# First gate/up tile decoded in the prologue, and the second norm rebuilt on transposes in two pairs of banks

## What is computed

```python
x = _layernorm(x + attention(x, weight_qkv, weight_proj))          # the "batch" axis of x is its second one
x = _layernorm(x + selective_scan(ctx_1024, z=x, in_proj_w, conv_w, conv_b, x_proj_w,
                                  dt_proj_w, dt_proj_b, A_log, D))
x = _layernorm(x + down(silu(gate(x)) * up(x)))
```

## Time and profile before

| | |
|---|---|
| median of 3 runs | 992.76 us (992.56 to 994.16) |
| profiled execution | 990.59 us, span 988.8 us |
| mean granted TensorE clock | 0.906 of full speed |
| busy: PE, DVE, ACT, POOL | 88%, 77%, 68%, 49% |

### The profile page before, as it was taken

The page is one execution under the profiler, slowest core; times in us unless marked ns, Lnnn a source line. Parts: engine busy times, 40 slices in busy tenths (PEclk is TensorE's granted clock), DMA queues, the critical chain, the costliest instruction groups (busy, mean ns, idle before and its releaser), DMA issues.

```text
span 988.8 us, 11890 instructions
## 1 busy us (share of the span) xinstructions
PE 869.3 (88%) x3824; PEld 626.4 (63%) x3824; DVE 765.2 (77%) x1066; ACT 672.4 (68%) x994; POOL 481.3 (49%) x445
## 2 busy tenths in 40 slices
PE   6879888787878897787989879899999999899997
PEld 3547654465544674456545457787777778688885
DVE  3797899877998879986788666888888888355442
ACT  4698985789956899668696464777777776242321
POOL 0079867799767998669676631221112111001000
PEclk9789777999779797787979988999999999899998
DMA  8167979589996799967999222111111110223221
GB/s 259 39 168 177 209 161 229 117 221 245 210 224 122 204 241 210 224 125 202 208 289 277 83 96 86 46 61 42 42 42 44 62 42 22 75 86 107 86 64 53
DMA packets 49908, 135.99 MB, mean 138 GB/s; under 512 B 5364, under 2 KB 13684, under 8 KB 41156
## 3 DMA queue, kind: packets, MB, share of 16 engines
q0 software_dynamic: 8064, 58.72, 30.9%
q1 hardware_dynamic: 40432, 76.44, 23.1%
q10 hardware_dynamic: 1364, 0.25, 0.2%
HBM read 57.93 MB, written 78.51 MB: 138 GB/s over the span
## 4 chain that ended last, share of the span: by engine, by line
PE 26%; issue 23%; DVE 23%; ACT 19%; POOL 5%; DMA 4%; DVEq 1%; ACTq 0%; POOLq 0%; SPq 0%
DVE state L1191 6%; PE banks L606 5%; ACT decay L893 5%; PE banks L720 5%; ACT scaled L882 5%; PE banks L744 4%; DVE leaf L1219 3%; DVE w_gu L1219 3%; PE banks L644 3%; PE banks L548 3%; DVE conv_in L1094 3%; POOL state L1442 2%; ACT leaf L1001 2%; DMA hT<-y_scratch 2%; DMA y_scratch<-state 1%
## 5 line engine op out<-in xcount | busy, mean ns | idle before, releaser
L1442 POOL TENSOR_TENSOR state<-state,crep 128x512 f32<-128x512 f32 x243 | 334.8, 1603 | 85.9 <-DVE state L1191 79.7
L1191 DVE TENSOR_TENSOR_SCAN state<-decay,banks 128x512 f32<-128x512 f32 x243 | 280.7, 1202 | 54.2 <-PE banks L644 44.6
L720 PE MATMUL banks<-x2T,wgu 128*128 128x512 f32 x1056 | 246.3, 393 | 4.8 <-DVE hT L1270 4.1
L644 PE MATMUL banks<-ident,scaled 128*128 128x128 f32 x1024 | 175.9, 314 | 69.1 <-DVE state L1191 49.7
L720 PEld LDWEIGHTS banks<-x2T,wgu 128*128 128x128 f32 x1056 | 197.9, 189 | 52.1 <-DVE hT L1270 11.3
L644 PEld LDWEIGHTS banks<-ident,scaled 128*128 128x128 f32 x1024 | 136.2, 161 | 143.1 <-DVE state L1191 63.4
L893 ACT ACTIVATE decay<-delta,negA 128x512 f32<-128x512 f32 x256 | 169.9, 722 | 77.6 <-DVE state L1191 69.8
L882 ACT ACTIVATE scaled<-duT,BT 128x512 f32<-128x512 f32 x256 | 163.8, 720 | 0.0
L1001 ACT ACTIVATE leaf<-idx_sb,table,table_gap 128x1024 f32<-128x1024 uint8 (+1 forms) x132 | 129.4, 1022 | 6.8 <-DVE w_down L1219 3.2
L1219 DVE COPY_PREDICATED leaf<-idx_sb,leaf 128x1024 f32<-128x1024 uint8 (+1 forms) x88 | 94.1, 1069 | 7.1 <-issue 6.1
L1534 POOL TENSOR_TENSOR pool_wait_here<-minus_half 128x1 f32<-128x1 f32 x22 | 4.3, 193 | 180.6 <-DVE w_gu L1219 116.2
(11 more groups left out here) (140 smaller groups left out, 1155.6 us busy)
## 6 DMA issues: line engine op xcount, KB each, us to landing
y_scratch<-state POOLq DMA_DIRECT2D x52, 1024.0 KB, 8.5
crep<-c_scratch SPq DMA_DIRECT2D x64, 256.0 KB, 5.4
idx_sb<-in_idx SPq DMA_DIRECT2D x11, 512.0 KB, 3.5
xT_sb<-in_xT SPq DMA_DIRECT2D x16, 256.0 KB, 4.8
y_scratch<-u SPq DMA_DIRECT2D x4, 1024.0 KB, 6.1
y_scratch<-state SPq DMA_DIRECT2D x4, 1024.0 KB, 6.3
leaf<-x_scratch SPq DMA_DIRECT2D x16, 256.0 KB, 2.8
out<-leaf SPq DMA_DIRECT2D x16, 256.0 KB, 2.0
```

Source lines behind the costliest of these rows:

```text
L644: last = nc.tensor.transpose(banks[:, k % NB, lc * LQ:(lc + 1) * LQ], scaled[:, g % SR, lc, et * P:(et + 1) * P], ident[:])
L720: last = mm(banks[:, 2 * tb + w, :], wgu[par][:, w, ws, t * P:(t + 1) * P], x2T[:, tb, xs, t, :], start=t == 0 and n == 0, stop=t == HT - ...
L1191: V.tensor_tensor_scan(state[:, g % GR, et, :], decay[:, k % DR_RING, :], banks[:, k % NB, :], 0.0, ALU.mult, ALU.add).then_inc(scan_ready, 1)
L1442: G.tensor_tensor(state[:, g % GR, et, :], state[:, g % GR, et, :], crep[:, g % CR, :], ALU.mult)\
```

## The change

- *Prologue.* SP loads the table first and the first index tile (0.5 MB) after xT, ahead of `wqkv`. POOL computes the table's gaps and then all eight leaves of gate/up tile 0 into the still unused `state`; DVE does the two bit operations after the taps of et 0 and 1, six selects before `softplus` and the seventh after it. SP stores the tile in DRAM (`w0_scratch`) and loads it back into `w_gu` when the scan's buffers are free. Before the in-projections PE runs four matmuls on zeros (`WARM`).
- *End of the scan.* The last row of y gets a place of its own (`y_last`, in `leaf`) and is loaded at n = 11, behind a wait for `y_out` and ahead of the last `repeat_c`; both index tiles leave that place.
- *Second norm.* `y_over` only transposes y (8 per half) into one pair of banks, 0 and 1 for the first four halves, 4 and 5 for the last four; DVE adds x1 from SBUF and takes the statistics there. `x2_over` has the pair 2 and 3, then 6 and 7. All four row gatings are DVE's. ACT copies half k before it applies half k + 1. The decode of tile 1 moves to the end of the stage, the first block of the FFN's first tile is cut in halves of 12 matmuls between the halves of the norm, and the silu and product of its first two blocks move ahead of the next decode.

The core of the diff (declarations and renumbered semaphores left out):

```diff
+                sp.dma_start(first_table, lut.to_broadcast([P, 16])).then_inc(first_lut_in, 16)
                 sp.dma_start(ip[:], ipT.rearrange("(t p) n -> p t n", p=P)).then_inc(ip_in, 16)
                 load_ctx(0)
                 load_xT(0)
+                sp.dma_start(first_words, idx[0, :, 0:2 * H]).then_inc(first_idx_in, 16)
                 sp.dma_start(wqkv[:], wqkvT.rearrange("(t p) n -> p t n", p=P)).then_inc(wqkv_in, 16)
...
+                        if n == 0 and b == 0:
+                            sp.wait_ge(first_mux_ready, 7)
+                            sp.dma_start(w0_scratch, first_leaf(0)).then_inc(first_stored, 16)
...
                         if b == S - 1 and n == 11:
                             sp.dma_start(table[:], lut.to_broadcast([P, 16])).then_inc(lut_in, 16)
-                            load_idx(*FIRST)
-                            load_idx(*SECOND)
+                            sp.wait_ge(y_out, 16)
+                            sp.dma_start(y_last, y_scratch[b].rearrange("(p t) l -> p t l", p=P)).then_inc(y_in[b], 16)
...
-                load_row(S - 1)
+                sp.dma_start(x1b[S - 1][:, 0:3, :], x1_scratch[S - 1].rearrange("(t p) h -> p t h", p=P)[:, 0:3, :])\
+                    .then_inc(x1_in[S - 1], 16)
+                sp.wait_ge(first_stored, 16)
+                sp.dma_start(w_gu[:].rearrange("p w n -> p (w n)"), w0_scratch).then_inc(first_in, 16)
+                load_idx(*SECOND)
+                load_idx("down", 0)
                 store_x2(0)
                 store_x2(1)
-                chunk_done(*FIRST)
-                load_idx("down", 0)
...
+                pe.wait_ge(zeros_ready, 1)
+                for _ in range(WARM):
+                    mm(banks[:, 7, :], state[:, 0, 0, 0:P], state[:, 0, 0, :], start=True, stop=True)
                 pe.wait_ge(ip_in, 16)
...
-                        mm(banks[:, half_bank(k, i), :], ident[:], x1_tile(b, lt), start=True, stop=False)
-                        for et in range(4):
-                            last = mm(banks[:, half_bank(k, i), et * P:(et + 1) * P],
-                                      yb[b][:, et, lt * P:(lt + 1) * P], ident[:], start=False, stop=et == 3)
-                        last.then_inc(sum_out, 1)
+                        if k % S:
+                            pe.wait_ge(x1y_ready, 2 * k - 1 + i)
+                        for et in range(ET):
+                            last = nc.tensor.transpose(banks[:, y_bank(k, i), et * P:(et + 1) * P],
+                                                       yb[b][:, et, lt * P:(lt + 1) * P], ident[:])
+                        last.then_inc(yT_out, 1)
...
-                residual(0)
-                residual(1)
-                for k in range(6):
-                    residual(k + 2)
+                y_over(0)
+                rest_summed()
+                y_over(1)
+                for k in range(2 * S):
+                    if k + 2 < 2 * S:
+                        y_over(k + 2)
                     x2_over(k)
-                gate_up(0, 0, (0,), first=True)
-                x2_over(6)
-                gate_up(0, 0, (1,), first=True)
-                x2_over(7)
+                    if 3 <= k < 7:
+                        gate_up(0, 0, ((k - 3) // 2,), first=True, halves=((k - 3) % 2,))
                 gate_up(0, 0, (2, 3), first=True)
...
                     for i, lt in enumerate(lts):
-                        A(x1b[b][:, lt, :], banks[:, half_bank(k, i), :], ACT.Identity, bias=shift[:, lt:lt + 1],
+                        A(x1b[b][:, lt, :], x1b[b][:, lt, :], ACT.Identity, bias=shift[:, lt:lt + 1],
                           scale=rstd[:, lt:lt + 1]).then_inc(x2_ready, 1)
...
+                for k in range(2 * S):
+                    x2T_hi(k)
+                    if k == 2:
+                        act.wait_ge(gap_ready, 1)
+                        act.wait_ge(ysum_out, ET * (DS * S - G0) + ET)
+                    if k in WITH_HALF:
+                        leaves(*SECOND, WITH_HALF[k])
+                    if k + 1 < 2 * S:
+                        norm_apply(k + 1)
+                leaves(*SECOND, (4, 5, 6))
+                silus(0, 0)
+                silus(0, 1)
                 high_part(1, 1)
...
                     for i, lt in enumerate(lts):
-                        dve.wait_ge(sum_out, 2 * k + i + 1)
-                        V.bn_stats(stats[:, lt, :], banks[:, half_bank(k, i), :]).then_inc(stat2_ready, 1)
+                        dve.wait_ge(yT_out, 2 * k + i + 1)
+                        V.tensor_tensor(x1b[b][:, lt, :], banks[:, y_bank(k, i), :], x1_tile(b, lt), ALU.add)\
+                            .then_inc(x1y_ready, 1)
+                    for i, lt in enumerate(lts):
+                        dve.wait_ge(x1y_ready, 2 * k + i + 1)
+                        V.bn_stats(stats[:, lt, :], x1b[b][:, lt, :]).then_inc(stat2_ready, 1)
...
+                first_selects(range(6))
                 softplus(0, (0, 1))
                 softplus(0, (2, 3))
+                first_selects((6,))
                 head_products(0, 3)
...
+                for j in range(8):
+                    G.tensor_tensor(first_wait[:, 8 + j:9 + j], minus_half[:, 0:1], minus_half[:, 0:1], ALU.add)
+                    G.tensor_scalar(first_leaf(j), first_bit(0), first_gap[:, j:j + 1], first_table[:, 2 * j:2 * j + 1],
+                                    ALU.mult, ALU.add).then_inc(first_leaf_ready, 1)
```

More of the change, by code:

```diff
@@ L161, in layer @@
         OWN_FROM = 3
+        WARM = 4
         DOWN = (3, 2, 1)
@@ L329, in loads_of @@
             if kind == "gate_up":
[L330 to L331 removed]
+                return f
+            return f + 1
         def wide(kind):
@@ L708, in x2_over, with gate_up @@
                             last.then_inc(x2T_out, 1)
-                def gate_up(f, par, blocks=range(TB), first=False):
+                def gate_up(f, par, blocks=range(TB), first=False, halves=range(2)):
                     pe.wait_ge(wlo_ready, f + 1)
@@ L713, in gate_up @@
                         if first:
-                            pe.wait_ge(x2lo_ready, 10 + 2 * tb)
+                            pe.wait_ge(x2lo_ready, 4 + 4 * tb)
+                            pe.wait_ge(x1y_ready, 8 + tb // 2 * 8)
                         else:
                             pe.wait_ge(h_ready, f * 4 - 3 + tb)
-                        for w in range(2):
+                        for w in halves:
                             for t in range(HT):
@@ L998, in leaves @@
                             act.wait_ge(mux_ready, q * 7 + LEAF_AFTER[j])
-                        elif not (kind == "gate_up" and first):
+                        elif not (kind == "gate_up" and isinstance(f, int) and f == 1):
                             act.wait_ge(mux_ready, q * 7 - 7 + LEAF_AFTER_LAST[j])
@@ L1271, in inner, with first_selects @@
                                     banks[:, 2 * tb + 1, :], ALU.mult).then_inc(h_ready, 1)
+                def first_selects(steps):
+                    for m in steps:
+                        kept, other, bit = FIRST_MUX[m]
+                        dve.wait_ge(first_leaf_ready, max(kept, other) + 1 if m < 6 and bit == 1 else 8)
+                        if m in (2, 5, 6):
+                            dve.wait_ge(first_mux_ready, m)
+                        V.memset(first_wait[:, m:m + 1], 0.0)
+                        V.copy_predicated(first_leaf(kept), first_bit(bit), first_leaf(other)).then_inc(first_mux_ready, 1)
                 V.memset(score[:], MASKED).then_inc(mask_ready, 1)
@@ L1338, in _ @@
                 single_bits(*SECOND)
[L1339 to L1342 removed]
+                norm_shift(3)
+                x2T_lo(2)
+                for k in range(5, 2 * S):
                     norm_stats(k)
[L1344 to L1348 removed]
+                    norm_shift(k - 1)
+                    x2T_lo(k - 2)
+                    if k > 5:
+                        select(*SECOND, (k - 6,))
@@ L1349, in _ @@
+                norm_shift(7)
                 x2T_lo(6)
+                select(*SECOND, (2, 3), then=("down", 0))
+                x2T_lo(7)
+                select(*SECOND, (4,))
+                inner(0, 0)
                 select(*SECOND, (5,))
-                x2T_lo(7)
+                inner(0, 1)
                 select(*SECOND, (6,))
@@ L1531, in last_leaf @@
                     pool.wait_ge(bits_ready, q + 1)
-                    if not (kind == "gate_up" and isinstance(f, int) and f == 0):
+                    if not (kind == "gate_up" and isinstance(f, int) and f == 1):
                         pool.wait_ge(mux_ready, q * 7)
```

207 lines of the change are left out of this document (110 added, 97 removed).

## The result

| | before | after |
|---|---|---|
| median (range) | 992.66 us (991.86 to 994.16), 4 runs | 1000.70 us (999.84 to 1004.38), 4 runs |
| profiled execution; span | 990.59; 988.8 us | 1001.52; 999.7 us |

The ratio is 1.0091, 95% interval 1.0071 to 1.0110: slower by 8 us, above the range of the prediction. The same kernel, timed again beside the experiments (e11_again), gave 1000.23 us and 1.0081 (1.0061 to 1.0102).

The account below looks back on a forecast made before the run. Bounds: TensorE's chain at the start, DMA at the scan's end, then the FFN's decode beat, so tile 1's copy start counts. +3.6 +1.2 -3.1 -1.3 = +0.4; 990.59 + 0.4 + 2.17 = 993.2 us; 8-in-10 range 986.0 to 998.0.

Parts of the forecast that it names:

- My bound of 1.37 us: Prologue: each of the two selects among GpSimd's leaves costs at most its own 1.37 us, staying inside the cover.
- the term +3.6: Prologue: k/v products start later and partly at half clock rate, delaying the x projection and the chain by 3.6 us.
- Rival 4: Prologue: GpSimd's leaves stretch beside VectorE's taps and selects, softplus starts 8.8 us late; 998.4 us, chance 0.06.
- +1.2 us: Scan's end: last row of C, behind the new wait with equal bytes ahead, comes 1.2 us later.
- rival 3: Scan's end: last row of C behind the new wait lands at 546, +5 instead of +1.2; 997.0 us, chance 0.10.
- my bound of +5: Scan's end: upper bound, if the queue gives the late megabyte no better share than it gave C's row.
- The term -3.1: Norm stage: the last select before the copy of gate/up tile 1 ends at 615.2, 3.1 us before 618.35.
- Rival 2: Norm stage: the decode's end does not move, last select at 618 or later; 996.3 us, chance 0.18.
- Rival 1: Norm stage: halves overlap, VectorE's 60 us decide, copy starts near 609; 985.9 us with the clock held, chance 0.30.
- the 66 to 76: Norm stage: forecast wrong if under 66 or over 76 us lie between last scan product and tile 1's copy.
- my -4.4: Norm stage and first FFN tile together: the forecast's -3.1 and -1.3 us.
- my "rows after holes": Prologue: profile rows where TensorE ran at half rate after idle holes, read as predicting half rate for k/v's first 3.7 us.

Follow-up runs that it names:

- e11_again: The changed kernel itself, unaltered, timed again beside the experiments; 1000.23 us, ratio 1.0081 to the kernel before.
- e6: Changed kernel with one more wait: VectorE starts the gatings of rows 0 and 1 only after GpSimd's last product; 996.60 us.
- e9: Changed kernel with the last row of C issued behind the wait for the y rows but ahead of the 1 MB load; 989.31 us.
- e8: Changed kernel without tile 0's decoding in the prologue (index load, bit operations, leaves, selects; tile set to zero, layer not computed); 995.96 us.
- e12: Changed kernel without tile 0's prologue decoding and with the last row of C ahead of the wait; layer not computed; 981.34 us.
- e1: Changed kernel with the last row of C issued ahead of SyncE's wait for the y rows instead of behind it; 988.15 us.
- e5: Changed kernel with the last row of C ahead of the wait and the second bit operation right behind the first; 984.57 us.
- e10: Kernel before the change, with the two index tiles issued behind the last row of C instead of ahead of it; 992.97 us.
- e7: Kernel before the change, with only a SyncE wait for the y rows added ahead of the last row of C; 992.20 us.

## Why the prediction was wrong, point by point

*Prologue, TensorE:* right in this execution, and in part by luck. wqkv's products start at 17.59 (forecast 17.8), take 7.10 (7.3), the x projection starts at 24.63 (25.3). But in e6 and e9, whose start is the same code, the clock held through a hole of the same length, and the x projection started at 23.02 and 22.96 (last section). What I counted as 24 k/v and 16 input matmuls are records; in f32 there are half as many matmuls, which changes no time.

*Prologue, VectorE and GpSimd: mis-sized by 1.4 to 2.5 us.* "The other four wait for the eighth leaf and end at 33.0" and "softplus' data come at 34.0, so they are hidden" were the steps. The second bit operation stands behind the taps of tile 1, so the leaves start at 17.3, not 16.4; beside the two early selects one leaf took 2.32 us instead of 1.20 and one small operation 1.24 instead of 0.20. My bound of 1.37 us for each of the two selects held (1.12 and 1.04 us lost); what was wrong is that this would stay inside the cover, since the four late selects wait for the last leaf. The eighth leaf ended at 30.2, not 27.5, and the last select at 35.5. VectorE then carried the delay on: the term +3.6 measured +5.0 at softplus and +4.8 (e11_again) to +5.95 at the row maximum in the traces, and 4.3 us (e8) to 6.8 us (e12) in medians. Rival 4 had the mechanism, for two of GpSimd's instructions and not for all.

*Last row of C: the step that failed.* "Bytes ahead are equal, only their start is later ... I take +1.2 us." Bytes ahead were equal, but before they had been issued some 6 us ahead of the row, which itself was issued at 518.5; now both start after the wait, at about 529.0 on before's clock (518.18 and the time that the sum of y was in flight, 10.7 us before, 11.0 in the change). The 1 MB took 12.0 us, where I had it landed at 537, 8 us after its issue; the row comes 5.7 us behind it (548.9, 554.6), about as it did behind the index tiles. On before's clock that is 529.0 + 12.0 + 5.7 = 546.7 against 541.0: +5.7, and VectorE's wait grew by as much (8.38 for 2.62). That is rival 3 (given 0.10), above its price and my bound of +5. The sum put the term at +1.2. The text's own condition, a scan's end beyond 549, names this step.

*What I left out: GpSimd's last products beside two gatings.* My walk started from state sums that end at 550.5, as before, 8.7 us after the last scan product. They end 11.0 us after it (555.33 to 566.3), since VectorE now has two gatings, row 0 as before and row 1 from GpSimd, right where the products run. e6 prices it at 3.6 us, e1 shows it gone when the row is in time. The earlier trace rows had shown the three products at 5.83 us, beside one gating.

*Norm stage, from the last state sum to the copy:* forecast 550.5 to 615.2, 64.7 us; measured 566.3 to 630.92, 64.6; before, 67.85. The term -3.1 was right once its start is given: the ten other traces of the rebuilt stage have 62.6 to 65.9. The walk holds too, 15.8 us later: second norm at 574.6 (forecast 559.0 + 15.8 = 574.8), the leaf that holds ScalarE until 595.5 (596.0), the fourth select behind the leaves at 622.94 (622.3), the end at 630.9 (631.0). One agreement in it is luck: the gating of row 2 ended 2 us earlier than I had it, and the shift stretched by GpSimd (2.30 for 0.15 us) took that back. Rival 2 (no gain) falls. Rival 1 (a dense transition, 67 us from the last scan product's end to the copy) is not reached, since the last leaves do hold the selects; but where C's row is in time the stretch is 71.3 us (e1: 544.80 to 616.11), 71.2 (e12), 70.9 (e9) and 69.2 (e5), 2 to 4 us below my 73.4 and between it and the rival; in the change it is 75.6, inside the 66 to 76 that I had set. *First FFN tile:* -1.0 for -1.3.

*Sum.* Of the 8 us, +4.3 are the prologue (e8) and +12.1 the row of C with the stretched products (e1); what is left for the norm stage and its tile is -8.4 (e12, measured by itself: -11). Each of these is good to some 3 us. I had +3.6, +1.2, -4.4. The last gain is larger than my -4.4. It counts from a scan without VectorE's wait of 2.62 us, and the late row of y is gone too, which e10 points to as a limit of its own; that these two make up the difference is argued, and how they share it was not measured.

## What to carry to other kernels

When a wait goes into an engine's DMA list, ask what the queue holds behind it, and issue the small transfer that others wait for ahead of the large one that the wait guards: here 0.25 MB behind 1 MB cost 11 us with all that followed, and changing places was enough. When work moves from GpSimd to VectorE, look at what GpSimd does at that moment and who waits for it: holding the gatings back made the kernel 3.6 us faster. Removing a wait in a trace says little until the next one that ends there (here a row of y) is named and undone as well.

## What the runs showed of the hardware

Two windows, first of the changed kernel, then of e9_crepmid, whose program is the same up to the scan's end (columns as in rows 4), with the k/v row of e9 (the changed kernel's is the fourth of the timeline at the start):

```profile
17.70:21.70 4.00, 4.00 (x11) 3.20 (x12) 3.86 (x7) 1.19 (x3) 4.00 (x7) 0.57 1.03 349
```
```profile
17.70:21.70 4.00, 4.00 (x19) 3.54 (x20) 3.86 (x7) 0.82 (x3) 4.00 (x7) 1.00 0.99 354
17.61 5.42 PE L564 MATMUL banks<-wqkv,xT_sb 128*128 128x256 f32 x24 [3.07 <-DMA wqkv<-in_wqkvT]
```

After the same input projections and nearly the same hole (2.68 and 3.07 us) TensorE had a granted clock of 0.57 in one execution, so mostly its lower level of 1.2 GHz, and of 1.00, 2.4 GHz, in the other; the same 24 records took 7.10 and 5.42 us. Of the five kernels with this same start, three took 7.10 or 7.11 us (changed, e11, e1; holes of 2.68, 3.34 and 2.99 us) and two 5.42 (e6, e9; 3.18 and 3.07). So neither the length of the hole nor my "rows after holes" decided it, and what did is open: the x projection's start varies by up to 1.9 us between executions that begin alike.

A small transfer issued behind a large one on SyncE's queue landed 5.6 to 5.9 us behind it, whether it was issued 5.5 us after it (before), 16 us (e7) or 0.4 us (changed, e11); issued ahead of it, it landed in 8.7 us (e9).

GpSimd and VectorE hardly overlap when both work from SBUF: three products take 3.74 us alone (e1) and two gatings 4.56, together 8.3; side by side they took 7.8 us, in turn 8.2 (e6). The exclusive port pair that the Trainium skill describes (SBUF — State Buffer, "Terms") fits this. The totals alone would fit a shared bandwidth as well, but the state sums show when each product ended: they start at 555.94, 559.22 and 562.50, 3.28 us apart. That is near one product and one gating alone in turn (1.25 + 2.28 = 3.5); with equal sharing a product would take twice its 1.25 us, so I would estimate 2.5.
